# Decoder block on one core: rotation scan started a round earlier in its own two tiles, steps cut finer, instruction order written anew

## The reference

```
h = layernorm(x)                                   # stage 1: gated delta rule
p = h @ cond_in_W;  s_t = R(theta) s_{t-1} + p_t   # 64 rotations, a scan over time
cond = rmsnorm(s) * w;  deltas = cond @ delta_W
q, k, v, decay, beta, gate = split(h @ ctrl_W + ctrl_b)   (+ ramp * deltas)
q, k, v = silu(causal_conv4(.));  q, k = l2norm
S = g*S + k (x) beta*(v - k.(g*S));  o = q.S       # scan over 1024 steps, 16 heads
x += (rmsnorm(o) * silu(gate)) @ Wo + bo
x += differential cross attention(layernorm(x), ctx of 64 keys)  # stage 2
x += conv3, 1x1 conv, silu, router, 8 experts (top 2), out, rmsnorm, ffn  # stage 3
```

## Time and profile before

| | us |
|---|---|
| median of 3 runs (lowest, highest) | 1598.05 (1592.85, 1598.37) |
| the profiled execution, its own time | 1595.61 |
| span from first to last instruction of it | 1593.8 |
| PE busy | 1479.4 (93%) |
| DVE busy | 1191.7 (75%) |
| ACT busy | 842.7 (53%) |
| POOL busy | 204.5 (13%) |
| mean granted clock of TensorE | 0.985 |

### The profile page before, as it was taken

One profiled execution on the slowest core, in us unless ns is written; L12 is line 12 of the kernel. 1 busy time (PEld: TensorE's weight loads), 2 busy tenths in 40 slices (PEclk: granted clock), 3 DMA queues, 4 the chain that ended last, 5 costly groups with the idle time before them and its releaser, 6 DMA issues.

```text
span 1593.8 us, 38771 instructions
## 1 busy us (share of the span) xinstructions
PE 1479.4 (93%) x16116; PEld 989.8 (62%) x16116; DVE 1191.7 (75%) x3193; ACT 842.7 (53%) x1606; POOL 204.5 (13%) x212
## 2 busy tenths in 40 slices
...
DMA packets 20214, 31.30 MB, mean 20 GB/s; under 512 B 1480, under 2 KB 17864, under 8 KB 19784
## 3 DMA queue, kind: packets, MB, share of 16 engines
...
...
## 4 chain that ended last, share of the span: by engine, by line
PE 71%; DVE 23%; ACT 3%; issue 3%; DVEq 0%
PE bank L1862 14%; PE bank L1449 6%; PE bank L1576 6%; PE bank L1810 4%; PE four L1661 3%; PE bank L1798 3%; PE bank L1577 3%; PE bank L1474 3%; PE bank L1778 3%; PE four L1713 2%; PE four L1729 2%; PE bank L1497 2%; DVE cs L1283 2%; PE four L1680 2%; PE bank L1481 2%
## 5 line engine op out<-in xcount | busy, mean ns | idle before, releaser
L1862 PE MATMUL bank<-w_sb,cs 128*128 128x512 f32 x512 | 245.9, 600 | 0.3 <-ACT cs L824 0.3
L824 ACT ACTIVATE cs<-bank 128x512 f32<-128x512 f32 x128 | 76.2, 595 | 162.0 <-PE bank L1455 140.6
L1862 PEld LDWEIGHTS bank<-w_sb,cs 128*128 128x128 f32 x512 | 94.3, 190 | 89.3 <-issue 82.4
L778 ACT COPY cs<-bank 128x512 f32<-128x512 f32 x116 | 67.5, 582 | 154.3 <-PE bank L1798 154.3
L544 POOL TENSOR_TENSOR decayed<-state,pk 128x512 f32<-128x512 f32 x64 | 69.5, 1086 | 618.7 <-DVE state L1196 618.7
L1810 PE MATMUL bank<-vx_sb,cs 128*128 128x136 f32 x896 | 118.0, 284 | 9.5 <-ACT cs L778 9.4
L1397 DVE SCALAR_TENSOR_TENSOR cs<-cs,rwt 128x256 f32<-128x256 f32 x224 | 100.1, 503 | 31.5 <-ACT cs L824 31.4
L1810 PEld LDWEIGHTS bank<-vx_sb,cs 128*128 128x128 f32 x896 | 109.4, 190 | 21.8 <-ACT cs L778 14.3
L1497 PEld LDWEIGHTS bank<-c_sb 128*128 128x128 f32 x796 | 96.9, 196 | 19.0 <-issue 13.2
L1497 PE MATMUL bank<-c_sb 128*128 128x128 f32 x796 | 101.4, 282 | 7.4 <-DMA c_sb<-in_consts 5.1
L1576 PE MATMUL bank<-hT,w_sb 128*128 128x512 f32 (+1 forms) x224 | 107.5, 602 | 0.4 <-ACT pre L622 0.2
...
## 6 DMA issues: line engine op xcount, KB each, us to landing
...
```

Of the source, the lines that this page charges most:

```text
L1862: mm(dst, x1T[:, k, b * TB:b * TB + TB], ew[:, k, ep * 512:ep * 512 + 512], start=k == 0, stop=False)
```

## The change

- `scan` and `unrot` write in place: the sum goes into `rota`, the cosine product into `rotb`, the turned state into `rota`, its square and the norm factor into `rotb`. `qkv[:, 0:3]` is no longer touched by them, so waits for block i's use of these tiles go from `scan` and `unrot`, and waits of the same kind are added to ACT's `proj.0`, `proj.2` and `proj.4`.
- `scan` and `unrot` are now `*` steps at the end of the round in front.
- Steps are cut finer: `max`, `conv`, `dconv`, `dsel`, `gsub`, `norm.2`, `norm.3`, `solve.0` and `solve.15` on DVE, `proj`, `qx`, `pv`, `wp`, `pw`, `mo` on PE, `gexp`, `mkq` and `silu` on ACT. The instructions are the same.
- `proj.j.0` (the two matmuls on `hT`) can stand well ahead of `proj.j.1` (the one on `rotb`), with the PSUM accumulation open in between. While it is open in rounds from 1 on, `keep` returns at once.
- All four lists and `KEEP` are written anew.

```diff
-                        last = V.tensor_tensor_scan(qkv[:, 2, lo_:hi_], rota[:, lo_:hi_], rotb[:, lo_:hi_], zc[:, b:b + 1], ALU.add, ALU.add)
+                        last = V.tensor_tensor_scan(rota[:, lo_:hi_], rota[:, lo_:hi_], rotb[:, lo_:hi_], zc[:, b:b + 1], ALU.add, ALU.add)
...
-                        tt(r3(rota[:, :]), r3(qkv[:, 2, :]), cosb, ALU.mult)
+                        ch1.link(tt(r3(rotb[:, :]), r3(rota[:, :]), cosb, ALU.mult))
...
-                    ch1.do(tt(r3(rotb[:, :]), r3(room(i, "unrot")[:, :]), sinb, ALU.mult))
-                    if i:
-                        dve.wait_ge(v_out.sem, v_out.at(i - 1, 16))
-                    fin("z", tt(qkv[:, 0, :], rota[:, :], rotb[:, :], ALU.subtract))
+                    ch1.wait()
+                    ch1.do(tt(r3(rota[:, :]), r3(room(i, "unrot")[:, :]), sinb, ALU.mult))
+                    fin("z", tt(rota[:, :], rotb[:, :], rota[:, :], ALU.subtract))
...
             def keep(i, count):
+                if i > 0 and used.get("open"):
+                    return
...
-                def proj(j):
+                def proj(j, part):
+                    if part == 0:
+                        controls(emptied("proj", j)[:, :], j * P, P, 0)
+                        used["open"] = 7 if i else FIRST["proj", j]
+                        return
                     up("cond")
-                    dst = emptied("proj", j)
-                    fin("proj_ps", controls(dst[:, :], j * P, P))
+                    fin("proj_ps", controls(room(i, "proj", j)[:, :], j * P, P, 1))
+                    here[0] = used.pop("open")
```

More of the change, by code:

```diff
@@ L116 @@
     "pe": steps('''
[L117 to L121, removed]
@@ L127 @@
-        -mo.1 co.6.0 d1.7 co.6.1 *turn1.0 cs.7.0 -ffd.0 cs.7.1 co.7.0 co.7.1 -turn6.1 -ffu.0 -ffd.1 *turn1.1 onorm.0
-        onorm.1 *rot.0 -ffu.1 wo.0 *rot.1 wo.1 *gate.0 wo.2 +sum.0 +sum.1'''),
-    "dve": steps('''
[L130 to L144, removed]
@@ L145 @@
-    "act": steps('''
[L146 to L154, removed]
+        decay +gate.1 sum.2 grow -turn2.0 sum.3 -turn2.1 -qx.0.0 -qx.0.1 +cond -sc.0.0 -qx.1.0 -qx.1.1 vturn -sc.0.1
```

350 lines of the change are left out of this document (213 added, 137 removed), and 6 rows, old and new, of the table KEEP.

## The result

The changed kernel takes 1524.94 us (median of 4 runs, 1519.54 to 1527.65), the kernel before 1596.34 beside it (4 runs). The ratio is 0.956, 95% interval 0.952 to 0.960: 71 us less, where 36 were forecast.

What follows compares the result with a forecast made beforehand. PE was taken as nearly full, with DVE bounding the front. Gains of 5.4 us in rounds 1 to 5, 4.2 in round 6 and 5 in round 0 made 36 us, giving 1562 us, range 1538 to 1594.

Steps and rivals of the forecast that it cites:

- middle and experts: From z.0 through the expert outputs: moved fillers and a later first weighted sum cost 2.0 and 1.5 us a round.
- The clock I leave: 0.: Whole kernel: no gain or loss counted from changes in PE's granted clock, 0 us.
- round 0: First round: 58 fewer identity matmuls, and scan and unrot leaving its solve; 2.3 us sure, 5 taken.
- the tail: Round's end: ln1.1 shortens from 3.38 to 1.6 us and turn1.0 stops waiting; credit 1.2 us, bounds -1 and +1.9.
- the front: Round's start to z.0: moved PE work fills idle time and replaces identity matmuls; credit 7.7 us a round.
- more than forecast: Rival: middle and experts cost nothing, no clock lost; 80 us gained at the very most, case time 1540 us, chance 0.13.
- The slower rival: Rival: without identity matmuls in rounds 1 to 6, new waits make the clock fall; 1612 us, chance 0.08.
- Its price of 0.4 us for each us at 1.2 GHz: Clock rival's rate: each us spent at the half-clock level costs about 0.4 us.
- DVE bounds that stretch: Front, 614 to 645 us: DVE, busy 29.9 of 31 us, sets the pace and PE waits for its steps.
- near 175: Sign of a right forecast: a steady round takes near 175 us at full clock.
- No PE wait over 0.3: Sign of a right forecast: no PE wait over 0.3 us between 34 and 58 us of a round.

Runs made afterwards that it cites:

- e9: Changed kernel with the pieces of every cut DVE and PE step side by side, no identity matmuls in rounds 1 to 6: 1604.17 us, ratio 1.006.
- e8: Kernel before with 17 more identity matmuls in each of rounds 1 to 6, at seven of PE's waits: 1585.85 us, ratio 0.995.
- e1: Kernel before with an empty KEEP, so none of its 398 identity matmuls runs: 1641.73 us, ratio 1.032.
- e2: Changed kernel with an empty KEEP, so none of its 275 remaining identity matmuls runs: 1548.71 us, ratio 0.974.
- e15: Kernel before with the identity matmul counts of round 0 halved (133 to 63): 1595.47 us, ratio 1.002.
- e3: Changed kernel's functions with the kernel before's lists and KEEP, cut pieces side by side, scan and unrot where they were: 1587.47 us, ratio 0.998.
- e4: As e3, but scan and unrot alone moved to the end of the round in front: 1600.55 us, ratio 1.006.
- e16: Changed kernel with 21 more identity matmuls in PE's waits of rounds -2, 0 and 7: 1525.30 us, ratio 0.957.
- e10: Changed kernel with db, proj.0 to proj.3, btr, brep and conv.0 back in the middle, no identity matmuls in rounds 1 to 6: 1675.46 us, ratio 1.053.
- e12: e4 with gate.1, cond, db, proj.0 to proj.2, btr, brep moved into the front, no identity matmuls in rounds 1 to 6: 1643.77 us, ratio 1.031.

## Why the prediction was wrong

The sign and most mechanisms held; four terms of the sum were mis-sized (middle and experts, the clock, round 0, the tail), and the diagnosis of the front was wrong. Of the rivals "more than forecast" came, given 0.13: 71 us, where its very most was 80. Idle time of PE in round 3, between the same events before and after:

| stretch | idle and identity before | after | gain | forecast |
|---|---|---|---|---|
| start to `z.0` | 4.91 + 3.33 | 1.41 | 6.8 | 7.7 |
| `z.0` to first expert | 0.57 | 1.32 | -0.75 | -2.0 |
| the experts | 0.09 | 0.33 | -0.24 | -1.5 |
| last expert to the end | 2.79 | 0.61 | 2.2 | 1.2 |
| sum | | | 8.0 | 5.4 |

The remaining 0.3 of the 8.3 us lies in the busy time of PE's other matmuls, 168.9 before and 168.6 after.

- **Middle and experts: the step that failed first.** Middle and experts were priced at 3.5 a round and cost 1.0. I took middles of bounds; PE's cut halves stand there between the chunks' links, and DVE's cut pieces let the links through. With the pieces side by side (e9) the middle's idle is 6.93 us in place of 1.32 (4.71 with DVE's alone, 3.88 with PE's), so the price I feared is that of the coarse steps. `conv.1` ahead of `top` delays nothing.
- **"The clock I leave: 0."** The old rounds 1, 2 and 5 paid 10.2 us to half-clock stretches, the new ones nothing. I had the 10 in the text and gave it to the rival "more than forecast" only. e8 gets these stretches away by filling waits, e1 makes more by emptying them, and e2 shows that the new lists need no filling: a full PE keeps its own clock. The slower rival fell for this reason. Its price of 0.4 us for each us at 1.2 GHz was right: 2.9, 3.0 and 4.3 us for 6.8, 6.8 and 10.2 in rounds 1, 2 and 5, 3.6 for 10.2 in e1. The Trainium skill, "TensorE: Matmul & The Clock Gate", section "HAM oscillation — how this bites in real kernels", cited for the rival, holds here in kind: waits let the clock fall (e1), and with the waits filled it stays up (e8). The page's own case has one long wait before each group of matmuls; here no wait of e1's round 3 was over 2.0 us, and it fell.
- **Round 0: 5 taken, 12.4 measured.** My reason (58 identity matmuls fewer, partly hidden) doesn't hold alone: e15 runs 70 fewer in the old order, and round 0 gets longer. What made the 12.4, order or placing, stays open. Real work on PE is 83.2 us before and 82.0 after; identity and waits with it fell from 44.4 to 33.3.
- **The tail: 1.2 taken, 2.2 measured.** `ln1.1` fell from 3.38 us to 1.38 (the forecast's 4 x 0.407 adds up instructions that overlap) and the 1.73 us wait with it. I left out the wait of 0.86 at `turn5.1` for the last weighted sum, now gone; a new one of 0.49 stands at `turn6.0`, for `hnorm`. In round 3 of e3 and e4 the 1.73 is missing too, but there `ln1.1` still takes 3.38 and `turn1.0` comes as late as before (161 us into the round): 3.4 us at 1.2 GHz just in front had taken the wait's place. That is no test of it.
- **The front: 7.7 taken, 6.8 measured,** `z.0` comes 61.1 us into the round by PE's first `decay` matmul, 60.6 by the forecast's count, which begins 0.4 us later (forecast 60.7). But "DVE bounds that stretch" was false. In the changed kernel DVE is nearly as busy there and PE waits a third as much (1.2 of 31 us, 3.85 before); e4 took DVE's load away, `z.0` came no sooner, and PE waited more. The waits were handovers, and other work of PE is what closes them. That the sum came out near is due to pricing the waits as filled.
- **The signs.** No L1532 records in full rounds, `ln1.1` short and the scan beside `wo`: as named. A round of "near 175" was 172.3. "No PE wait over 0.3" there fails by little: 0.42 and 0.38 stand.

The excess of 36 us over the forecast is then: rounds 1 to 5 at full clock 5 x 2.9 = 14.5, the clock of rounds 1, 2 and 5 10.0, round 0 7.4, round 6 4.8, rounds 7 and 8 3.0, less 4.0 in the head, 35.7. The 10.0 is for the profiled execution and differs between executions. In the head the clock falls to 1.2 GHz for 6.8 us near the end of a wait of 3.63 us for the first scan; e16 fills it and gets 2.7 back.

Open: how low stretches in round 0 move between kernels whose lists there are the same (e16), and how much of the rounds' gain is the fillers' and how much the rest of the lists, since each alone loses (e10, e12); and what POOL's and ACT's lists are worth by themselves, which no run changes alone.
